# Ternary feed-forward weights turned by SyncE's DMA transposes during the retention instead of by TensorE at the feed-forward's opening

## The reference, cut to what matters

```
# retention, after scores, mask and A (one A for all batches)
O = einsum('hst,bthe->bshe', A, V);  Y = groupnorm(O)
x = x + (relu(x @ wg) * Y) @ wo

# feed-forward: w1, w3 are 1408 x 512, w2 is 512 x 1408
act_quant(x)    = clip(round(x * 127/max|x|), -128, 127) / scale
weight_quant(w) = clip(round(w / mean|w|), -1, 1) * mean|w|
h = silu(bitlinear(x, w1)) * bitlinear(x, w3)
x = x + bitlinear(h, w2)
```

## Time and profile before

| | us |
|---|---|
| median of 3 runs | 1227.72 (1226.38 to 1228.2) |
| span of the profiled execution | 1223.2 |
| median less span (start and end around the first and last instruction) | 4.5 |
| feed-forward's opening, to the first `up` matmul | 246.6 to 261.65 |
| PE busy | 1108.5 (91% of the span) |

### The profile page before, as it was taken

How to read it: one execution, slowest core, us unless ns; L and a number is a source line. 1 busy time by engine, 2 the same in 40 slices (tenths; PEclk the granted TensorE clock), 3 DMA queues, 4 the chain that set the end, 5 groups by cost and what they waited for, 6 DMA issues and landing times. The chain is left out here.

```text
span 1223.2 us, 22308 instructions
## 1 busy us (share of the span) xinstructions
PE 1108.5 (91%) x6266; PEld 835.1 (68%) x6284; DVE 845.2 (69%) x1628; ACT 511.3 (42%) x1067; POOL 402.8 (33%) x323
## 2 busy tenths in 40 slices
PE   6999799978888599999989997999999999999997
PEld 5989676544444257898878664776777776777773
DVE  3548447878886655787887994767677677666646
ACT  1332134266666247888722162333333333333330
POOL 0000001111110020466764001556666556566630
PEclk9999899999999898998989997999999999999999
DMA  7324330010000058765156413878789898778659
GB/s 263 146 109 163 127 131 1 0 19 1 0 0 1 35 178 282 259 240 189 45 198 222 82 52 120 233 188 219 181 228 246 197 235 224 185 186 190 140 98 378
DMA packets 98716, 183.29 MB, mean 150 GB/s; under 512 B 13513, under 2 KB 31305, under 8 KB 98672
## 3 DMA queue, kind: packets, MB, share of 16 engines
q1 hardware_dynamic: 81040, 144.41, 35.1%
q0 software_dynamic: 17632, 38.32, 15.9%
HBM read 136.56 MB, written 50.34 MB: 153 GB/s over the span
## 5 line engine op out<-in xcount | busy, mean ns | idle before, releaser
L2377 POOL DMA_INDIRECT y_d<-tail,x_ox x78 | 167.3, 2144 | 134.5 <-ACT tail L2604 105.4
L2449 PE MATMUL x_h<-x_w_hi,x_t_hi 128*128 x320 | 127.9, 400 | 2.3 <-DVE x_t_lo L2618 2.3
L2450 PE MATMUL x_h<-x_w_lo,x_t_hi 128*128 x320 | 127.7, 399 | 0.0
L2451 PE MATMUL x_h<-x_w_hi,x_t_lo 128*128 x320 | 127.4, 398 | 0.0
L1662 POOL DMA_INDIRECT e_rows<-r_d,x_ix x80 | 85.0, 1063 | 125.2 <-issue 107.8
L2618 DVE TENSOR_TENSOR x_w_lo<-w,x_w_hi (+1 forms) x64 | 109.6, 1753 | 2.6 <-ACT x_w_hi L2575 2.6
L2566 ACT ACTIVATE e_rows<-x_h 128x256 f32<-128x256 f32 x80 | 30.8, 384 | 184.0 <-PE x_h L2451 184.0
L211 POOL TENSOR_TENSOR ln_rstd<-ln_ve,powers 128x2 f32<-128x2 f32 (+1 forms) x40 | 26.2, 655 | 245.6 <-DVE ln_ve L205 245.6
L2618 DVE TENSOR_TENSOR x_t_lo<-x_xb,x_t_hi 128x512 fp32r<-128x512 f32 x80 | 55.2, 692 | 42.2 <-ACT x_t_hi L2561 42.2
L1542 DVE SCALAR_TENSOR_TENSOR h_c<-h_qk,h_d 128x768 f32<-128x768 f32 x64 | 58.2, 952 | 26.2 <-PE h_qk L1436 14.4
L2468 PE MATMUL x_o<-x_w_hi,x_avt_hi 128*128 x160 | 71.5, 447 | 1.6 <-issue 1.3
(11 more groups left out here) (435 smaller groups left out, 2667.4 us busy)
## 6 DMA issues: line engine op xcount, KB each, us to landing
w<-in_L_ffn_w SPq DMA_DIRECT2D x32, 1024.0 KB, 7.7
w<-in_L_ffn_w SPq DMA_DIRECT2D x32, 512.0 KB, 9.8
h_negm<-negm_d SPq DMA_DIRECT2D x15, 1024.0 KB, 6.9
raw<-in_L_ffn_w SPq DMA_DIRECT2D x3, 2816.0 KB, 16.3
x_res<-in_x SPq DMA_DIRECT2D x8, 512.0 KB, 4.7
ctx_in<-in_ctx SPq DMA_DIRECT2D x8, 512.0 KB, 3.7
kt_d<-ct SPq DMA_DIRECT2D x8, 512.0 KB, 3.1
vc_d<-ctx_in SPq DMA_DIRECT2D x8, 512.0 KB, 2.6
```

Source lines behind the costliest of these rows:

```text
L2377: nc.gpsimd.indirect_dma_start(out=y_d[s], out_offset=bass.IndirectOffsetOnAxis(ap=ox[q][:, s:s + 1], axis=0), in_=eo[q][s][:], in_offset= ...
L2449: nc.tensor.matmul(hbank[s], hi[:, k, :], w13p[0][:, at, k, :], start=k == 0, stop=False)
L2450: nc.tensor.matmul(hbank[s], hi[:, k, :], w13p[1][:, at, k, :], start=False, stop=False)
L2451: last = nc.tensor.matmul(hbank[s], lo[:, k, :], w13p[0][:, at, k, :], start=False, stop=k == KD - 1)
```

## The change

- The opening's 132 turns, their four PSUM buffers' semaphores and the 22 copies on ACT and DVE are removed.
- SP turns the matrices by 26 DMA transposes from SBUF to SBUF, in the retention's second half: 11 for `w1` (128 x 512 each), 11 for `w3`, 4 for `w2` (128 x 1408 each). They stand behind `load_raw` in SP's list. `w1`'s wait for batches 0 to 2 of `pv`; `w3`'s for batches 0 to 5 and for DVE's pieces 1 and 2; `w2`'s for pieces 3 and 4.
- The destinations are memory that is no longer read: `w1t` and `w3t` lie over `v_rows`, `w2t` over `raw`. `v_rows` is allocated outside the retention.
- DVE's four pieces are now half a matrix each (2816 columns of one): two of `w3`, then two of `w2`. They count up `tern_ready`. Batches 3 to 6 on DVE are written out instead of looped.
- In tile 0 of the feed-forward PE waits for `w1_in`, `w3_in` and `w2_in` before the first use of each.

```diff
+class Turned:
+    def __init__(self, sem, raw, vt):
+        n = KF * D
+        dead = vt[:].rearrange("p t d -> p (t d)").bitcast(BF16)
+        self.w1t, self.w3t = (dead[:, n * j:n * (j + 1)].rearrange("p (k f) -> p k f", k=KD) for j in range(2))
+        self.w2t = raw[:].bitcast(BF16)[:, 0:n].rearrange("p (f d) -> p f d", f=KF)
+        self.first_batch_past = [-(-n * (j + 1) // (2 * CB * D)) for j in range(2)]
+        self.w1_in, self.w3_in, self.w2_in = (sem(f"{n}_turned_in") for n in ("w1", "w3", "w2"))
+        self.turns = {"w1": KF, "w3": KF, "w2": KD}
...
@@ retention, second half, SP
             load_raw(sp, 2, raw2)
+            def turn_up(name, dst, done, j):
+                sp.dma_start_transpose(dst[:, :, j * P:(j + 1) * P], tern[name][:, j * D:(j + 1) * D]).then_inc(done, 16)
+
+            def turn_down(m):
+                sp.dma_start_transpose(turned.w2t[:, :, m * P:(m + 1) * P],
+                                       tern["w2"][:, m * F0:(m + 1) * F0]).then_inc(turned.w2_in, 16)
+
+            sp.wait_ge(o_ps, CB * turned.first_batch_past[0])
+            for j in range(KF):
+                turn_up("w1", turned.w1t, turned.w1_in, j)
+            sp.wait_ge(o_ps, CB * turned.first_batch_past[1])
+            sp.wait_ge(tern_ready, 1)
+            for j in range(KF // 2):
+                turn_up("w3", turned.w3t, turned.w3_in, j)
+            sp.wait_ge(tern_ready, 2)
+            for j in range(KF // 2, KF):
+                turn_up("w3", turned.w3t, turned.w3_in, j)
+            for half in range(2):
+                sp.wait_ge(tern_ready, 3 + half)
+                for m in range(KD // 2 * half, KD // 2 * (half + 1)):
+                    turn_down(m)
...
@@ retention, second half, DVE
-            part = KF * D // (B - 1 - QUIET)
+            part = KF * D // 2
+            def piece_of(n):
+                return [(1, raw), (2, raw2)][n // 2:n // 2 + 1], n % 2 * part, part
+
+            def ternary_piece(n):
+                (j, src), = piece_of(n)[0]
+                cols = ds(n % 2 * part, part)
+                steps.settle()
+                nc.vector.tensor_scalar(tern[names[j]][:, cols], src[:, cols], -1.0, None, ALU.max).then_inc(tern_ready, 1)
...
@@ feed-forward, PE
-        for n, (pieces, _) in enumerate(jobs):
-            if n >= NB:
-                pe.wait_ge(wt_sb[n % 2], (n - NB) // 2 + 1)
-            for j, piece in enumerate(pieces):
-                last = nc.tensor.transpose(turning[n % NB][:, j, :], piece, identb[:])
-            last.then_inc(wt_ps, 1)
-        for e in range(2):
-            pe.wait_ge(wt_sb[e], (len(jobs) + 1 - e) // 2)
...
+            if first:
+                pe.wait_ge(turned.w1_in, 16 * turned.turns["w1"])
             up(par, g_bank, w1t, g_ps, range(3))
...
+            if first:
+                pe.wait_ge(turned.w3_in, 16 * turned.turns["w3"])
             up(par, u_bank, w3t, None, range(2))
...
-            if not first:
+            if first:
+                pe.wait_ge(turned.w2_in, 16 * turned.turns["w2"])
+            else:
                 down(t - 1)
...
@@ feed-forward, ACT and DVE: the same steps of the first tokens, without the copies
-        weight_copies(0, 6)
         normal(0)
-        weight_copies(6, 12)
         grid_x(0)
-        weight_copies(12, 18)
         normal(1)
-        weight_copies(18, len(jobs))
         copy_x(0, 0)
```

More of the change, by code:

```diff
@@ L156, in program @@
             tern = {n: sbuf(st, f"tern_{n}", [P, KF * D], BF16) for n in ("w1", "w3", "w2")}
+            raw = sbuf(st, "raw", [P, KF * D])
+            vt = sbuf(st, "v_rows", [P, NT, D])
             w_mean = sbuf(st, "w_mean", [P, 3])
-            raw = sbuf(st, "raw", [P, KF * D])
+            turned = Turned(sem, raw, vt)
             with ExitStack() as sr:
-                retention(nc, sr, sem, sbuf, psum, a, x, x_rows, ctx_rows, ident, powers, tern, w_mean, raw, kt_d, vc_d, upto)
+                retention(nc, sr, sem, sbuf, psum, a, x, x_rows, ctx_rows, ident, powers, tern, w_mean, raw, vt, turned, kt_d, vc_d, upto)
             if upto >= 2:
-                bit_ffn(nc, st, sem, sbuf, psum, a, x, ident, powers, tern, w_mean, early)
+                bit_ffn(nc, st, sem, sbuf, psum, a, x, ident, powers, turned, w_mean, early)
         clear_semaphores()
@@ L212, in power, with retention @@
                                      powers[:, 0:1].to_broadcast([P, lanes]), ALU.pow).then_inc(self.rstd_ready, 1)
-def retention(nc, st, sem, sbuf, psum, a, x, x_rows, ctx_rows, ident, powers, tern, w_mean, raw, kt_d, vc_d, upto):
-    vt = sbuf(st, "v_rows", [P, NT, D])
+class Turned:
[7 more added lines that the diff above has]
+        self.turns = {"w1": KF, "w3": KF, "w2": KD}
+def retention(nc, st, sem, sbuf, psum, a, x, x_rows, ctx_rows, ident, powers, tern, w_mean, raw, vt, turned, kt_d, vc_d, upto):
     wt = sbuf(st, "gate_t", [P, KD, T])
@@ L647, in means, with batch @@
                                         ALU.max).then_inc(mean_sb, 1)
-            def batch(b, piece=None, last_piece=None):
+            def batch(b, piece=None):
                 gate(b)
-                if last_piece is not None:
-                    normalise(b + 1, between=lambda: to_bf16(steps, weights, last_piece * part, part))
+                if piece:
+                    normalise(b + 1, between=lambda: ternary_piece(piece - 1))
                 else:
                     normalise(b + 1)
-                if piece is not None and last_piece is None:
+                if piece == 0:
                     means()
@@ L658, in batch @@
                 if piece is not None:
-                    if last_piece is None:
+                    if piece == 0:
                         dve.wait_ge(mean_ready, 2)
-                    to_grid(steps, weights, piece * part, part)
+                    to_grid(steps, *piece_of(piece))
                 residual(b, 1)
                 if piece is not None:
-                    off_grid(steps, weights, piece * part, part)
+                    off_grid(steps, *piece_of(piece))
             normalise(0)
@@ L668, in _, with bit_ffn @@
                 batch(b)
-            batch(QUIET, piece=0)
-            with steps.loop(0, B - 2 - QUIET, 10) as i:
-                batch(i + QUIET + 1, piece=i + 1, last_piece=i)
+            for b in range(QUIET, B - 1):
+                batch(b, piece=b - QUIET)
             gate(B - 1)
-            to_bf16(steps, weights, (B - 2 - QUIET) * part, part)
+            ternary_piece(B - 2 - QUIET)
             for c in range(CB):
                 residual(B - 1, c)
[L678 to L683, removed]
+def bit_ffn(nc, st, sem, sbuf, psum, a, x, ident, powers, turned, w_mean, early):
+    w1t, w3t, w2t = turned.w1t, turned.w3t, turned.w2t
     identb = sbuf(st, "identb", [P, P], BF16)
@@ L704, in bit_ffn @@
     tab, tbb = (t[:].bitcast(BF16).rearrange("p (k n) -> p k n", n=P) for t in (ta, tb))
-    turning = [tab, tbb] + [g_bank[:, n, :].bitcast(BF16).rearrange("p (k n) -> p k n", n=P) for n in range(2)]
-    NB = len(turning)
     KA = 8
@@ L722, in bit_ffn @@
                                 "hq_ready", "hta_ps", "htb_ps", "hta_sb", "htb_sb", "o_ps", "x_added"))
[L724 to L734, removed]
     block = st.enter_context(nc.Block())
@@ L997, in tile @@
                 integers_x(t + 2)
[L999 to L1004, removed]
         moments(0)
-        weight_copies(0, 10)
         spread_x(0, 0)
         moments(1)
-        weight_copies(10, 16)
         integers_x(0)
-        weight_copies(16, len(jobs))
         spread_x(1, 1)
```

5 lines of the change are left out of this document (1 added, 4 removed).

## The result

The changed kernel took 1220.28 us (median of 9 runs, 1216.06 to 1225.48) beside 1227.06 us (9 runs) for the kernel before: ratio 0.9949, 95% interval [0.9926, 0.9972]. The forecast of 1224.5 us and the lower end of its range, 1222, lie above it. The two kernels differ by 6.8 us in the medians and by 5.8 us in the means (standard error 1.4), about twice the 3.2 us that were forecast. Two more comparisons gave 5.5 and 4.4 us between the means (standard error 1.0 each). All 35 runs of the changed kernel have a mean of 1220.7 us (standard deviation 3.2), the 113 runs of the kernel before in the five sets of comparisons one of 1225.7 us (2.2): 5.0 us less, 95% about 3.8 to 6.1. The baseline on which the forecast stood, 1227.72, was the median of three runs and 2.0 us above that mean.

What follows compares the result with a forecast made beforehand. The prediction took the feed-forward's opening to hold back one chain behind `hidden(0)`; starting that 3.2 us earlier, with all added work counted as 0, gave 1227.7 - 3.2 = 1224.5 us, range 1222 to 1232.

Steps and rivals of the forecast that it cites:

- the sum's 3.2 us: Feed-forward's opening: `hidden(0)` starts at 263.4 instead of 266.61, a gain of 3.2 us, with nothing lost elsewhere.
- 12 x 0.43 = 5.2 us: Tile 0: `up` with `w1t` as 12 matmuls of 512 columns at half clock, ending at 260.4.
- The tokens' chain: Feed-forward's opening: without turns and copies, the first tokens' steps let the first `up` matmul start 6.4 us earlier, at 255.2.
- the full-clock case: Rival in tile 0: TensorE's clock stays full or returns early, gain 5.2 us, 1222.5 us; chance 0.10.
- Issue: Retention's end: SP's last two transposes take 2.00 us each to issue, within the 2.8 us available; slip 0.
- the middle row: Of three measured issue times, 0.64, 2.00 and 3.86 us, the 2.00 us one, taken for SP's transposes.
- Transfer: Retention's second half: at 16.4 ns a packet the DMAs take 17.3 us in all, `w2t` in place about 245; all hidden.
- Contention: Retention's second half: DMA transfers beside PE's reads in the `wo` groups cost 0.
- DVE's larger pieces: Retention: DVE's moved pieces, 1.7 us each, may hold POOL's reciprocal root back by up to 0.7 us; cost 0.
- SP holds the end: Rival at the block's end: SP's late issues delay the block change, 1226.6 us, or 1232 at 7.7 us each; chance 0.18.
- Slow transfers: Rival: transposes land one after another at 1.28 us a block, `down(0)` 63 us later, 1291 us; chance 0.12.
- Nothing comes of it: Rival: half clock lasts to tile 0's end (gain 0.6 us) or a later stage gives time back, 1227 us; chance 0.10.

Runs made afterwards that it cites:

- e2_both: The changed kernel's retention with its 26 DMA transposes, unread, followed by the old opening with all 132 turns on TensorE: 1226.43 us, ratio 1.0009.
- e3_no_turns: The changed kernel without any turns; the feed-forward multiplies by the unturned ternary matrices and computes other numbers: 1218.63 us, ratio 0.9942.
- e4_warm: The changed kernel with 24 idle TensorE matmuls before `turn_x(0)` and 5 behind it, to keep the clock up: 1219.61 us, ratio 0.9961.
- e6_hold: The changed kernel with six more DMA transposes behind the last one, into memory nobody reads: 1228.24 us, ratio 1.0032.
- e7_serial: The changed kernel with SP waiting after each DMA transpose until it has landed: 1224.42 us, ratio 0.9987.

## Why the prediction was wrong

**Right: the mechanism.** The gain arises in tile 0 alone, PE waits for no DMA, the first product runs at half clock, the clock is back 5.8 us after the first `up` matmul (forecast: by 5.6), and PE still releases `hidden(0)`. e2_both shows no cost of the adding side, and e3_no_turns that nothing more was to be had there.

**Wrong: the size of the gain.** The failing term is the sum's 3.2 us: `hidden(0)` at 263.4, which is 16.6 us after the statistics, against 19.81 before. It measured 20.12 - 16.07 = 4.0 us, and 4.25 from the first statistics to the mLSTM's. These parts make up the 0.8 us:

- `up` with `w1t` was counted as "12 x 0.43 = 5.2 us". Only 8 of the 12 are 512 columns wide; the last four are 384, since 1408 = 2 x 512 + 384. By form, in the changed kernel (behind the first bar the busy us and the mean ns of one, each of which overlaps the next, then the idle time before):

```profile
L839 PE MATMUL g_bank<-v_rows,f_xqt 128*128 128x512 bf16 x8 | 3.6, 631 | 1.6 <-ACT f_xqt L909 1.6
L839 PE MATMUL g_bank<-v_rows,f_xqt 128*128 128x384 bf16 x4 | 1.5, 527 | 0.0
```

  8 x 0.43 + 4 x 0.32 = 4.7 us, and `turn_x(1)` starts 4.67 us after the first. With that, the start of `w3t` was 5.09 us after the first `up` instead of 5.6: 0.5 us.
- The tokens' chain: the first `up` stood 8.05 us after the statistics, not 8.4. Of this 0.22 us is the step from the copy's end to the matmul, counted as the 0.28 of before and now 0.06; the rest is ACT's instructions overlapping each other by a tenth.
- Against it, the clock was still at half when `w3t` began, so that `hidden(0)` came 2.93 us after it instead of 2.6: 0.3 us.
- The one profile of before had tile 0 at 19.81 us; three others had 20.12. That is 0.3 us more gain.

**Wrong: the base and its spread.** The forecast took 3.2 us off 1227.7, the median of three runs. The mean over 113 is 1225.7. So of the 3.8 us between the forecast and the changed kernel's mean, 2.0 are the base, 0.8 the term above, and 1.0 is left. For the last, the profiles show no place: 0.25 us of it is the last `down`, and behind the mLSTM's start the two kernels differ by 0.6 us in the mean of profiles that spread by 5 to 8 us. With a standard error of 0.6 us on the 5.0 it may be chance. The range was built from bounds of the mechanism only, with nothing for the base; its lower end, 1222, was the full-clock case seen from 1227.7. The same 5.2 us from 1225.7 give 1220.5, which holds the mean of 1220.7 barely and the median of 1220.28 not. The upper end is mis-added as well: two issues of 7.7 us end at 240.7 + 15.4 = 256.1, a slip of 9.8 us, so that rival gives 1234.3 and not 1232.

**The terms on SP.** *Issue:* taken 2.00 us each, measured 1.37 to 1.65 us for `w2`'s. The slip of 0 held, with 2.7 us of room; it would have held with the row of 0.64 us too, so the choice of the middle row is not confirmed by it. The estimate from the Trainium skill, 2.35 us ("DMA: Bandwidth & Descriptors", "Why a DMA increments its semaphore by 16 and not by 1"), comes out too high for 88 tiles; and since 32 tiles (128 x 512) took 1.27 us, most of an issue does not go with the number of tiles. *Transfer:* taken 16.4 ns a packet, measured 20.4; `w2t` landed at about 241.4 + 3.8 = 245.2 (forecast 245). *Contention:* the 128 `wo` matmuls were busy 56.4 us on the pages of both kernels: none. *DVE's larger pieces:* they kept POOL's root back a little (the waits of `gn_y` for it are 5.8 us in all, 4.0 before). PE's waits for `gn_y` stayed at 3.6 us, but its wait before the last `wo` group grew from 2.60 to 2.75 us. So the term that the prediction put at 0 is 0.15 us, and the four profiles in which the clock fell behind that wait took 1.7 us more there. Whether the two belong together is open; e2_both bounds the whole at 3 us.

**The rivals.** *Full clock:* it did not happen by itself. Forced in e4_warm, it gave the bound in tile 0 (5.5 us to 20.12, forecast 5.2), and the time did not follow it. *SP holds the end:* not in this kernel; e6_hold and e7_serial show that the mechanism is real and costs about one for one, and SP would have to be busy 2.7 us longer than it is before it set in. *Slow transfers:* refuted. `w1`'s 44 blocks went in 11 issues of 1.27 us, 0.32 us a block, so the Trainium skill's 1309 ns for a block turned by DMA ("VectorE: DVE Perf Modes", "The three transpose paths") does not hold as a rate here; with a wait after each (e7_serial) the landing of four blocks is 2.4 us, 0.6 us a block. *Nothing comes of it:* refuted by three comparisons.

## What to carry to other kernels

- Work that an engine does at a stage's opening while the stage's own chain waits is worth moving to a queue that is idle earlier; what it brings is then the distance between the old wait and the chain's own pace, here 4 us of the 6.8 us by which the first matmul moved up, since TensorE came back from its idle stretch at half clock.
- When a gain of a few tenths of a per cent is forecast, the base deserves as much care as the terms: three runs of a kernel that spreads by 10 us fix it to no better than 1 or 2 us, and that belongs into the range.
- Count matmuls by form, not by group: a group's label shows one shape for all.

## What the runs showed that I had not expected

- A DMA transpose of four 128 x 128 blocks (bf16, SBUF to SBUF) took SP 1.27 us to issue, one of eleven blocks 1.48 us. Landing took 2.5 and 3.7 us. The long form is the cheaper one by far for a block: 0.13 us of issue against 0.32.
- Time won with the clock is partly lent. With idle matmuls tile 0 was 1.4 us shorter, the last `down` of the same stage 0.75 us longer; with the table load moved as well, 0.8 us more, and a fall of the clock in tile 1 that cost 1.4 us.
- The same kernel took from 1215.5 to 1227.0 us. Half-clock stretches fall at other places from execution to execution, and the mLSTM alone took 195.3 to 201.3 us. What decides this remains open.
- PE's idle stretch of 2.60 us before the last `wo` group was never followed by a fall of the clock (five profiles); with 2.75 us it was in four of twelve, for 1.7 us each time. Whether the 0.15 us decide that is not shown, but where a change lengthens a wait of TensorE the granted clock behind it is worth a look.
